# Two-level Strassen product with LoRA: M6 ahead of M7, T2 of the last four batches found early, U3 summed in SBUF

## The chip, the cores and the metric

One core of a Trainium2 chip runs the whole kernel. The metric is device time in microseconds (us), median of several runs.

## The reference, cut to what matters

```
# x (8, 512, 2048) f32; L0: A, B (8 adapters, rank 16); L1: W (2048, 2048), lora_A, lora_B (16 adapters, rank 16)
h = x + (x @ B0[i0].T) @ A0[i0].T          # per batch b: i0 = itok_B_3_7[b]
y = h + h @ W + (h @ A1[i1]) @ B1[i1]      # per batch b: i1 = itok_B_0_15[b]
```

The kernel computes y as x (I + W) plus low-rank terms, in f32 accuracy by splitting each operand in a high and a low part (w_hi, w_lo, b_hi, b_lo) with three matmuls for each product.

## The kernel before, in words

The product x (I + W) is found by the Winograd form of Strassen's method, with seven block products in place of eight. Batches are paired, so that the two batches of a pair stand side by side as the block matrix X11, X12, X21, X22 (half of the inner dimension, batch).

**First part (`one_level`), batches 0 to 3.** Two pairs p = 0, 1, each with products P1, P2, P6, P7, P4, P3, P5, each of 8 units. Unit n runs 24 matmuls (30 in P1, P2, P7, P4 of p = 0, which also find low-rank terms). All engines go through the same loop over n in their own queues. For unit n + 1 ScalarE casts the weight tile to `w_hi` (line 768) once TensorE has left unit n - 1, then VectorE finds `w_lo` (line 926); TensorE needs `w_lo` at the end of unit n. In the same way x is split (lines 779, 939). VectorE also adds the products up (line 987 and others) and forms sums of weights for the second part (`job_sum`, lines 1084 to 1094). SyncE issues loads in a written order: `load_raw` and `load_weights` for weights, `load_x` for x (X12 of pair 1 in P7 of pair 0). The four x tiles `x_raw[X11..X22]` each hold 8 chunks of 128x512.

**Second part (`two_level`), batches 4 to 7.** The four batches are multiplied by a two-level scheme: seven outer products in the order M1, M2, M7, M6, M4, M3, M5, each of seven inner products Q1 to Q7 in 14 units. Each outer product has an x block of four quarters `xq0` to `xq3` (1 MB each). For M7 the quarters are T3 = X12 - X22, for M6 T2 = T3 - X11, for M4 T2 + X21, for M5 T2 + X22. They are found by `first_diff` (line 2155), two adds or subtractions of 128x1024 for a quarter, from `xq` and a tile `tmp`; both are loaded by SyncE (`load_x`, line 1921, and `load_tmp`, line 1961). Three quarters are summed in the last units of the outer product ahead, the last one (quarter index 1) in unit 0. So that M6 can read T3 and M4 and M5 can read T2, GpSimd stores them to HBM (`store_t`, line 1856: `t3_kept`, three quarters, `t2_kept`, four).

Outer results: M1 begins U in `uq`, M2 is added in `stage` and stored. M7 is copied from PSUM by ScalarE into `stage` (line 2030, ten copies), the rest of its quarters added by VectorE (line 2214), and stored to two places of y (lines 1821, 1822). M6 is taken into `uq` (line 2211), and U2 is then added to the same two places of y by accumulating DMAs (`store_u2`, line 1834, 16 of 512 KB). M4 and M5 go the same way from `stage` (line 1825).

Weights come by `load_w` (line 1940), 1 MB for each inner product, two tiles in turn.

The order that the change touches is set by these lines:

```
M1, M2, M7, M6, M4, M3, M5 = range(7)
def x_kept(mo, i):   return i == 3 and mo in (M6, M4, M5)
def x_worked(mo, i): return mo in (M7, M6, M4, M5)
def by_act(q, begins): return begins and product(q)[0] in (M1, M7, M4, M5)
```

Of the kernel before, what the change touches and what calls it, by code (L numbers as in the profile page):

```python
# [43 lines left out]
M1, M2, M7, M6, M4, M3, M5 = range(7)  # L44
# [46 lines left out]
def one_level(nc, ctx, own, shared, xT, A0n, B0, W, A1, B1, yT):  # L91
# [176 lines left out]
    w_sum, w_ops, lrw, g_kept = shared.w_sum, shared.w_ops, shared.lrw, shared.g_kept  # L268
# [63 lines left out]
    job_summed = sem("job_summed")  # L332
    presum_done = sem("presum_done")
# [126 lines left out]
    def gpsimd(pool, early):  # L460
# [81 lines left out]
        for n in range(LAST + 1):  # L542
# [35 lines left out]
            if n in j_load_at:  # L578
                load_j(j_load_at[n])
            early(n)  # L580

    def sync(sp, early):
        def load_x(p, i, j):
            if p and i == X21:
                sp.wait_ge(w_ready, unit(0, P5, 4 + j) + 1)
                sp.wait_ge(f_stored[j], 16 * 4)
            elif p:
                user = {X11: P5, X12: P7, X22: P3}[i]
# [67 lines left out]

        def load_weights(n):
# [49 lines left out]
        for n in range(-1, LAST + 1):  # L707
# [188 lines left out]
    def vector(dve, early):  # L896
# [48 lines left out]
        def t3(p, j):  # L945
            dve.wait_ge(x_loaded[X12][j], 16 * (p + 1))
# [130 lines left out]

        def job_sum(o, k, e):
# [19 lines left out]
        for n in range(-1, LAST + 1):  # L1098
# [206 lines left out]
    part.g_stored = g_stored  # L1305
    part.u2_stored, part.u3_stored, part.stage_stored, part.stage_plan = u2_stored, u3_stored, stage_stored, stage_plan
# [6 lines left out]
def two_level(nc, ctx, own, shared, first, xT, B0, W, A1, yT):  # L1313
# [93 lines left out]
    def by_act(q, begins):  # L1407
        return begins and product(q)[0] in (M1, M7, M4, M5)
# [70 lines left out]
    for e, (mo, i, j) in enumerate(tmp_plan):  # L1479
        when = max(when, tmp_when[e - TMPS] if e >= TMPS else when, (unit(M6, 3) if mo in (M4, M5) else 0, 0))  # L1480
# [47 lines left out]
    j_split_at = {unit(M7, 12): 0, unit(M6, 1): 1, unit(M3, 11): 2, unit(M5, 0): 3}  # L1528
# [18 lines left out]
    t3_kept, t2_kept = (nc.dram_tensor(name, (4, P, 2, 2, N), F32).ap() for name in ("t3_kept", "t2_kept"))  # L1547
# [38 lines left out]
    x_stored = [sem(f"x_stored{i}") for i in range(4)]  # L1586
# [121 lines left out]
    def added_before(q, t, count, c, begins):  # L1708
# [5 lines left out]
        base = {M2: M1, M6: M1, M3: M6}.get(mo)  # L1714
# [48 lines left out]
    def gpsimd(pool):  # L1763
# [48 lines left out]
        def store_stage(mo, c, h):  # L1812
# [10 lines left out]
            else:  # L1823
                pool.wait_ge(u_stored[c], 16 * 4)
# [3 lines left out]
        def store_u2(c, h):  # L1828

            m = 4 * (c // 2) + 2 * h + 8  # L1830
            pool.wait_ge(*quarter_done(M6, c, 2 * h + 1))
            pool.wait_ge(stage_stored[GROUP[M7][c]][h], 16 * stage_stores(M7, c, h))
            for pair in (1, 0):
                pool.dma_start(y_at(batch(pair, c % 2), m), uq[:, c, 2 * h:2 * h + 2, :], accum_op=ALU.add
                               ).then_inc(u_stored[c], 16)
# [38 lines left out]
        def rest():  # L1874
            for n in range(LAST + 2):
# [4 lines left out]
                store_sums(early_sums(n))  # L1880
# [10 lines left out]
                store_sums(late_sums(n))  # L1891
# [5 lines left out]
                for i in range(len(lr_plan)):  # L1897
                    if n == (lr_split_of[i - 2] + 1 if i > 1 else unit(M7, 4 + 2 * i)):
# [4 lines left out]
    def sync(sp):  # L1903
        def load_x(mo, i):
# [12 lines left out]
            if mo == M6:  # L1917
                sp.wait_ge(x_stored[i], 16 * t_stores(M7, i))
                src = t3_kept[c]
# [22 lines left out]
        def load_tmp(e):  # L1942
# [33 lines left out]
        def rest():  # L1976
# [18 lines left out]
            for c in range(4):  # L1995
                sp.wait_ge(u_stored[c], 16 * 6)
# [130 lines left out]
    def vector(dve):  # L2127
# [17 lines left out]
        def first_diff(mo, i):  # L2145

            for j in range(2):
                if x_kept(mo, i):
                    dve.wait_ge(*x_split_done(product_at(mo - 1, Q3)))
                    if mo == M4:  # L2150
                        dve.wait_ge(x_stored[i], 16 * t_stores(M6, i))
                else:
# [3 lines left out]
                                         ALU.subtract if mo in (M7, M6) else ALU.add)  # L2156
            last.then_inc(x_summed, 1)

        def x_diff(kind, mo):
# [8 lines left out]
            if mo in (M7, M6) and kind != "t1":  # L2168
                dve.wait_ge(x_stored[dst], 16 * t_stores(mo, dst))
# [22 lines left out]
        def evict(q, t, count, c, begins):  # L2192
# [248 lines left out]
def lora_residual_program(nc, xT, ids0, ids1, A0n, B0, W, A1, B1, yT):  # L2441
# [4 lines left out]
    with ExitStack() as ctx:  # L2446
# [13 lines left out]

        shared.eye = sb("eye", [P, P])
# [85 lines left out]
```

## Time and profile before

| | |
|---|---|
| median of 3 runs | 1356.53 us (1356.39 to 1359.65) |
| the profiled execution | 1358.25 us |
| its span | 1356.3 us |
| TensorE busy | 1303.0 us (96%) |
| VectorE, ScalarE, GpSimd busy | 947.6, 459.1, 175.9 us |
| DMA | 321.57 MB, 237 GB/s over the span |

The span runs from the first to the last instruction. Engines in the rows: PE is TensorE, PEld its weight loads, DVE VectorE, ACT ScalarE, POOL GpSimd, SP SyncE. PEclk is the share of TensorE's full clock that was granted. "idle before" is how long an engine stood still ahead of an instruction, and what released it.

### The profile page before, as it was taken

To read this page: it belongs to the slowest core of one execution; us is meant where nothing else is said; L and a number is where in the kernel's file an instruction comes from. 1 tells how busy PE (TensorE), PEld (TensorE's weight loads), DVE (VectorE), ACT (ScalarE), POOL (GpSimd) and SP (SyncE) were. 2 spreads that over 40 slices of the span, in tenths; PEclk is the share of its full clock that TensorE was granted. 3 is DMA by queue.
4 is the path that set the end of the run, shared out by engine and by line. 5 is a ranking of instruction groups with operands and counts; after the bars stand their busy time and mean duration, and the time that the engine had idled before them with its cause. 6 is when DMAs were issued, how large, how long until landed. Compare 5 with 4: busy or idle time off the path is not lost.

```text
span 1356.3 us, 15438 instructions
## 1 busy us (share of the span) xinstructions
PE 1303.0 (96%) x5684; PEld 1070.4 (79%) x5684; DVE 947.6 (70%) x1025; ACT 459.1 (34%) x536; POOL 175.9 (13%) x304
## 2 busy tenths in 40 slices
PE   5999999998999999999999999999999889999996
PEld 4878888887878788878887888888888668888785
DVE  4454764455686876776578767886798767778995
ACT  2331232222332422232232443334444335443451
POOL 4100100011023110001202000011112200110022
PEclk8999999998999999999999999999999989999998
DMA  8873854368998965556978473598899997877377
GB/s 308 282 263 128 282 182 133 106 205 274 324 366 290 329 216 210 184 181 215 303 247 307 133 259 125 191 356 273 307 358 300 281 258 199 237 165 230 102 210 163
DMA packets 87823, 321.57 MB, mean 237 GB/s; under 512 B 15796, under 2 KB 15796, under 8 KB 80452
## 3 DMA queue, kind: packets, MB, share of 16 engines
q1 hardware_dynamic: 59188, 237.00, 51.1%
q0 software_dynamic: 28560, 83.58, 22.1%
q8 instruction: 46, 0.75, 0.2%
q14 instruction: 29, 0.24, 0.1%
HBM read 207.19 MB, written 114.36 MB: 237 GB/s over the span
## 4 chain that ended last, share of the span: by engine, by line
PE 68%; DVE 12%; DMA 12%; issue 3%; ACT 2%; SPq 1%; POOL 0%; DVEq 0%; POOLq 0%; ACTq 0%
PE ps L1266 31%; PE ps L2423 29%; PE ps L1239 2%; DMA w_sum<-w_raw 2%; PE ps L2379 2%; DMA wq<-w_ops 2%; DMA w_raw<-in_W 2%; DMA xq<-in_xT 2%; PE ps L1197 1%; ACT w_hi L768 1%; DMA x_raw<-in_W 1%; DVE w_lo L926 1%; DVE xq L2170 1%; DVE w_lo L2183 1%; DVE x_raw L912 1%
## 5 line engine op out<-in xcount | busy, mean ns | idle before, releaser
L1266 PE MATMUL ps<-b_hi,w_hi 128*128 128x512 f32 x896 | 351.8, 393 | 17.0 <-DVE w_lo L926 15.3
L1266 PE MATMUL ps<-b_lo,w_hi 128*128 128x512 f32 x896 | 350.4, 391 | 0.0
L1266 PE MATMUL ps<-b_hi,w_lo 128*128 128x512 f32 x896 | 350.0, 391 | 0.0
L2423 PE MATMUL ps<-b_hi,w_hi 128*128 128x512 f32 x784 | 308.6, 394 | 15.4 <-DVE w_lo L2183 12.7
L2423 PE MATMUL ps<-b_lo,w_hi 128*128 128x512 f32 x784 | 307.3, 392 | 0.0
L2423 PE MATMUL ps<-b_hi,w_lo 128*128 128x512 f32 x784 | 307.0, 392 | 0.0
L1266 PEld LDWEIGHTS ps<-b_hi,w_hi 128*128 128x128 f32 x896 | 169.4, 189 | 55.5 <-DVE w_lo L926 17.9
L1266 PEld LDWEIGHTS ps<-b_hi,w_lo 128*128 128x128 f32 x896 | 169.3, 189 | 35.6
L1266 PEld LDWEIGHTS ps<-b_lo,w_hi 128*128 128x128 f32 x896 | 169.3, 189 | 35.1
L2423 PEld LDWEIGHTS ps<-b_hi,w_hi 128*128 128x128 f32 x784 | 148.4, 189 | 50.0 <-DVE w_lo L2183 14.8
L2423 PEld LDWEIGHTS ps<-b_hi,w_lo 128*128 128x128 f32 x784 | 148.5, 189 | 31.3
L2423 PEld LDWEIGHTS ps<-b_lo,w_hi 128*128 128x128 f32 x784 | 148.6, 190 | 30.7
L2012 ACT CAST w_hi<-wq 128x1024 fp32r<-128x1024 f32 x98 | 103.2, 1053 | 188.7 <-PE ps L2423 165.2
L2183 DVE TENSOR_TENSOR w_lo<-wq,w_hi 128x1024 fp32r<-128x1024 f32 x98 | 119.5, 1220 | 57.5 <-ACT w_hi L2012 56.9
L926 DVE TENSOR_TENSOR w_lo<-w_raw,w_hi 128x1024 fp32r<-128x1024 f32 x48 | 58.7, 1224 | 101.5 <-ACT w_hi L768 101.3
L768 ACT CAST w_hi<-w_raw 128x1024 fp32r<-128x1024 f32 x48 | 50.6, 1054 | 218.9 <-PE ps L1239 112.9
L2189 DVE TENSOR_TENSOR b_lo<-xq,b_hi 128x1024 fp32r<-128x1024 f32 x98 | 119.5, 1219 | 5.8 <-ACT b_hi L2020 5.3
L2020 ACT CAST b_hi<-xq 128x1024 fp32r<-128x1024 f32 x98 | 102.9, 1050 | 43.5 <-DVE xq L2170 18.3
L768 ACT CAST w_hi<-x_raw 128x1024 fp32r<-128x1024 f32 x31 | 32.7, 1053 | 134.6 <-PE ps L1266 79.8
L926 DVE TENSOR_TENSOR w_lo<-x_raw,w_hi 128x1024 fp32r<-128x1024 f32 x31 | 38.0, 1224 | 52.3 <-ACT w_hi L768 52.3
L939 DVE TENSOR_TENSOR b_lo<-x_raw,b_hi 128x1024 fp32r<-128x1024 f32 x56 | 68.2, 1217 | 0.0
L2170 DVE TENSOR_TENSOR xq<-xq 128x2048 f32<-128x2048 f32 x28 | 63.9, 2282 | 0.0
(174 smaller groups left out, 1268.2 us busy)
## 6 DMA issues: line engine op xcount, KB each, us to landing
w_raw<-in_W SPq DMA_DIRECT2D x63, 512.0 KB, 6.7
wq<-w_ops SPq DMA_DIRECT2D x28, 1024.0 KB, 6.1
xq<-in_xT SPq DMA_DIRECT2D x44, 512.0 KB, 6.7
out_y<-stage POOLq DMA_DIRECT2D x40, 512.0 KB, 8.8
x_raw<-in_xT SPq DMA_DIRECT2D x32, 512.0 KB, 7.3
w_raw<-w_sum SPq DMA_DIRECT2D x25, 512.0 KB, 6.1
wq<-w_sum SPq DMA_DIRECT2D x12, 1024.0 KB, 8.7
out_y<-uq POOLq DMA_DIRECT2D x24, 512.0 KB, 14.1
```

What stands on the lines that cost most here:

```text
L768: act.copy(w_hi[n % 2][:, :, :], w_tile(n)[:, :, :]).then_inc(w_hi_done, 1)
L926: dve.tensor_tensor(w_lo[n % 2][:, :, :], w_tile(n)[:, :, :], w_hi[n % 2][:, :, :].bitcast(F32), ALU.subtract).then_inc(w_ready, 1)
L939: dve.tensor_tensor(b_lo[:, 2 * j:2 * j + 2, :], x_raw[i][:, 2 * j:2 * j + 2, :], b_hi[:, 2 * j:2 * j + 2, :].bitcast(F32), ALU.subtract). ...
L1239: last = pe.matmul(p_ps[:, :], a0[:, 2 * j + c, :], w[n % 2][:, c, :], start=(j == 0 and c == 0 and k == 0), stop=(j == 3 and c == 1 and k ...
L1266: last = pe.matmul(bank[:, :], w[n % 2][:, c, t * P:(t + 1) * P], x[:, 2 * j + c, :], start=(j == 0 and c == 0 and w is w_hi and x is b_hi ...
L2012: act.copy(w_hi[:, h, :, :], w_half(q, h)).then_inc(w_hi_done, 1)
L2020: act.copy(b_hi[:, 2 * (q % 2) + j, :, :], xq[x_use(q)[0]][:, j, :, :]).then_inc(x_hi_done, 1)
L2170: dve.tensor_tensor(xq[dst][:, :, :, :], xq[a][:, :, :, :], xq[b][:, :, :, :], ALU.subtract).then_inc(x_summed, 1)
L2183: dve.tensor_tensor(w_lo[:, h, :, :], w_half(q, h), w_hi[:, h, :, :].bitcast(F32), ALU.subtract).then_inc(w_ready, 1)
L2189: dve.tensor_tensor(b_lo[:, slot, :, :], xq[x_use(q)[0]][:, j, :, :], b_hi[:, slot, :, :].bitcast(F32), ALU.subtract).then_inc(x_ready, 1)
L2379: last = pe.matmul(lr_ps, cols, x[:, 2 * (q % 2) + c // 2, c % 2, :], start=(begins and c == 0 and x is b_hi), stop=(ends and c == 3 and x ...
L2423: last = pe.matmul(out, w[:, h, c, col:col + P], b[x], start=(po in (Q1, Q2, Q5, Q3) and c == 0 and i == 0), stop=(c == 3 and i == 2), ski ...
```

## The change

The diff does these things:

- The outer order is M1, M2, M6, M7, M4, M3, M5.
- T2 = X12 - X22 - X11 of batches 4 to 7 is found in the first part, in eight pieces of 128x1024 (`late_t2`), five in X12's tile during P7 of pair 0 (after units 25, 27, 28, 30 and 31) and three in X21's tile in P4 and P3 of pair 1 (after units 90, 93 and 96). A piece has three loads of 512 KB by SyncE, two subtractions by VectorE at the end of its loop body, and one store to `t2_kept` by GpSimd.
- Pair 1's X12 is loaded in P4 of pair 0, not in P7.
- M6 loads its four quarters from `t2_kept` as they are. M7 loads three quarters and keeps the fourth (T2 + X11). M4 now loads all four. `t3_kept`, `store_t` and its seven stores are gone.
- M7's ten beginning copies on ScalarE become VectorE adds of `uq`: `stage` = U2 + M7 = U3, stored twice as before. `store_u2` and its 16 accumulating DMAs are gone.

```diff
-M1, M2, M7, M6, M4, M3, M5 = range(7)
+M1, M2, M6, M7, M4, M3, M5 = range(7)
...
+    LATE_T2 = [(X12, unit(0, P7, 1)), (X12, unit(0, P7, 3)), (X12, unit(0, P7, 4)), (X12, unit(0, P7, 6)),
+               (X12, unit(0, P7, 7)), (X21, unit(1, P4, 2)), (X21, unit(1, P4, 5)), (X21, unit(1, P3, 0))]
...
+        def store_late_t2(s):
+            i, _ = LATE_T2[s]
+            pool.wait_ge(late_t2_summed, 2 * s + 2)
+            pool.dma_start(t2_kept[s // 2, :, s % 2, :, :], x_raw[i][:, 2 * (s % 2):2 * (s % 2) + 2, :]
+                           ).then_inc(late_t2_stored[s % 2], 16)
...
+            elif k == 0:
+                sp.wait_ge(late_t2_stored[j], 16 * (s // 2))
+            else:
+                sp.wait_ge(late_t2_summed, 2 * (s - 1) + k)
+            half, pair = ((0, 1), (1, 1), (0, 0))[k]
+            src = xT[4 + 2 * pair + s // 2 % 2, 2 * half + s // 4, :, s % 2, :, :]
+            sp.dma_start(x_raw[i][:, 2 * j:2 * j + 2, :], src).then_inc(x_loaded[i][j], 16)
...
-                if o == P7 and 2 <= u < 6:
-                    load_x(p + 1, X12, u - 2)
+                if (o, u) in ((P4, 1), (P4, 2), (P4, 3), (P4, 4)):
+                    load_x(p + 1, X12, (2, 0, 3, 1)[u - 1])
...
+        def late_t2(s):
...
+                    dve.wait_ge(x_loaded[i][j], came + 16 * late_t2_uses(i, j, s))
...
+                dve.tensor_tensor(tiles[0], tiles[0], tiles[k], ALU.subtract).then_inc(late_t2_summed, 1)
...
-        return i == 3 and mo in (M6, M4, M5)
+        return i == 3 and mo in (M7, M5)
...
-        return mo in (M7, M6, M4, M5)
+        return mo in (M7, M4, M5)
...
-        return begins and product(q)[0] in (M1, M7, M4, M5)
+        return begins and product(q)[0] in (M1, M4, M5)
...
-        base = {M2: M1, M6: M1, M3: M6}.get(mo)
+        base = {M2: M1, M6: M1, M7: M6, M3: M6}.get(mo)
...
-                        if qmo == M6:
-                            store_u2(c, t // 2)
...
-                src = t3_kept[c]
+                for j in range(2):
+                    sp.wait_ge(first.late_t2_stored[j], 16 * (first.LATE_T2S // 2))
+                src = t2_kept[c]
```

How the rows of the queues move, at three places. First VectorE's queue from the last unit of P7 into P4 of pair 0 (`u` is the tile that sums products up, `q` a low-rank sum). Before:

```order
L926 TENSOR_TENSOR w_lo<-w_raw,w_hi 128x1024
L939 TENSOR_TENSOR b_lo<-x_raw,b_hi 128x1024
L1004 TENSOR_TENSOR a_lo<-lr_raw,a_hi 128x256
L987 TENSOR_TENSOR u<-ps,u 128x512 x4
L1062 TENSOR_TENSOR q<-ps,q 128x512
L921 TENSOR_TENSOR w_raw<-w_raw,eye 128x128 x2
L926 TENSOR_TENSOR w_lo<-w_raw,w_hi 128x1024
```

Now:

```order
L974 TENSOR_TENSOR w_lo<-w_raw,w_hi 128x1024
L987 TENSOR_TENSOR b_lo<-x_raw,b_hi 128x1024
L1052 TENSOR_TENSOR a_lo<-lr_raw,a_hi 128x256
L1035 TENSOR_TENSOR u<-ps,u 128x512 x3
L1136 TENSOR_TENSOR x_raw<-x_raw 128x1024 x2
L1035 TENSOR_TENSOR u<-ps,u 128x512
L1110 TENSOR_TENSOR q<-ps,q 128x512
L969 TENSOR_TENSOR w_raw<-w_raw,eye 128x128 x2
L974 TENSOR_TENSOR w_lo<-w_raw,w_hi 128x1024
```

The two subtractions of piece 4 stand ahead of a partial sum, the low-rank sum and the weights' split for unit 33.

Second, SyncE's queue through P7 of pair 0. Before:

```order
L625 DMA w_raw<-w_sum 128x1024 x5
L591 DMA x_raw<-in_xT 128x1024
L625 DMA w_raw<-w_sum 128x1024
L591 DMA x_raw<-in_xT 128x1024
L625 DMA w_raw<-in_W 128x1024
```

Now:

```order
L653 DMA w_raw<-w_sum 128x1024 x3
L699 DMA x_raw<-in_xT 128x1024 x3
L653 DMA w_raw<-w_sum 128x1024 x2
L699 DMA x_raw<-in_xT 128x1024 x3
L653 DMA w_raw<-w_sum 128x1024
L653 DMA w_raw<-in_W 128x1024
L699 DMA x_raw<-in_xT 128x1024 x3
L653 DMA w_raw<-in_W 128x1024
L699 DMA x_raw<-in_xT 128x1024 x3
```

Each single x load gave way to three, with waits on the piece ahead, between the weight loads.

Third, GpSimd's queue in the second part, from the end of M7 into M6 before:

```order
L1821 DMA out_y<-stage 128x1024
L1822 DMA out_y<-stage 128x1024
L1856 DMA t_kept<-xq 128x2048
L1821 DMA out_y<-stage 128x1024
L1822 DMA out_y<-stage 128x1024
L1834 DMA out_y<-uq 128x1024 x2
L1789 DMA lr_raw_q<-lrw 128x1x512
```

and from M6 into M7 now:

```order
L1868 DMA j_raw_q<-g_kept 16x4x16 x4
L1898 DMA out_y<-fix 128x1024 x2
L1847 DMA lr_raw_q<-lrw 128x1x512
L1898 DMA out_y<-fix 128x1024 x2
L1879 DMA out_y<-stage 128x1024
L1880 DMA out_y<-stage 128x1024
```

The stores of `xq` and `uq` are gone. The two stores of each `stage` pair now come in the block just ahead of M4.

## Rows read from the trace of the kernel before

**Rows 1.** The page: engine totals, and TensorE's busy tenths in 40 equal slices.
```profile
PE 1303.0 (96%) x5684; PEld 1070.4 (79%) x5684; DVE 947.6 (70%) x1025; ACT 459.1 (34%) x536; POOL 175.9 (13%) x304
...
PE   5999999998999999999999999999999889999996
```

**Rows 2.** Busy time by stretch: length, each engine's us (instructions), PEclk, DMA share, GB/s.
```profile
182.00:242.00 60.00, 60.00 (x266) 49.68 (x265) 30.77 (x39) 15.34 (x20) 1.12 (x2) 1.00 0.38 124
604.00:660.00 56.00, 54.85 (x242) 45.40 (x243) 35.92 (x39) 14.83 (x17) 10.35 (x20) 1.00 0.75 246
905.00:990.00 85.00, 84.51 (x373) 69.63 (x373) 64.76 (x63) 35.79 (x42) 12.01 (x22) 1.00 0.82 296
990.00:1060.00 70.00, 69.29 (x305) 56.80 (x304) 64.24 (x62) 32.10 (x39) 16.59 (x24) 1.00 0.98 312
1060.00:1080.00 20.00, 19.11 (x85) 15.49 (x83) 14.85 (x17) 5.06 (x5) 6.11 (x7) 1.00 1.05 285
1080.00:1100.00 20.00, 14.36 (x51) 11.58 (x52) 13.71 (x12) 7.38 (x8) 0.72 (x1) 0.74 1.05 284
1100.00:1120.00 20.00, 16.26 (x60) 12.88 (x59) 10.13 (x9) 5.74 (x6) 1.73 (x2) 0.83 0.89 244
1120.00:1140.00 20.00, 20.00 (x90) 16.55 (x89) 14.33 (x16) 11.13 (x15) 0.71 (x1) 1.00 0.60 182
```

**Rows 3.** Waits from 1068 to 1125 us: who waited for what, total, times, longest.
```profile
PE ps L2423 <- DVE w_lo L2183: 10.3, 2, 6.5
ACT w_hi L2012 <- DMA wq<-w_ops: 10.2, 1, 10.2
ACT b_hi L2020 <- DVE xq L2155: 9.8, 1, 9.8
DVE xq L2155 <- DMA xq<-in_xT: 5.9, 1, 5.9
```

**Rows 4.** The chain that ended last, within 1065 to 1095 us: start, length, what.
```profile
1061.72 20.35 DMA xq<-in_xT
...
1085.61 21.71 DMA wq<-w_ops
```

**Rows 5.** DMA issues from 1060 to 1110 us: how many, KB each, median us to landing.
```profile
out_y<-uq POOLq DMA_DIRECT2D x7, 512.0 KB, 28.8
tmp<-t_kept SPq DMA_DIRECT2D x4, 512.0 KB, 19.9
```

**Rows 6.** DMA issues from 900 to 985 us, and all that they moved.
```profile
DMA packets 5880, 25.17 MB, mean 296 GB/s; under 512 B 1027, under 2 KB 1027, under 8 KB 4595
...
out_y<-stage POOLq DMA_DIRECT2D x14, 512.0 KB, 9.7
tmp<-in_xT SPq DMA_DIRECT2D x8, 512.0 KB, 7.4
```

**Rows 7.** Groups by line and shape, whole span: total us, mean ns, idle before.
```profile
L2155 DVE TENSOR_TENSOR xq<-xq,tmp 128x1024 f32<-128x1024 f32 x32 | 37.6, 1217 | 5.9 <-DMA xq<-in_xT 5.9
...
L2214 DVE TENSOR_TENSOR stage<-ps,uq 128x1024 f32<-128x1024 f32 x6 | 7.3, 1220 | 5.0 <-PE ps L2423 5.0
```

**Rows 8.** VectorE's timeline, P7 into P4 of pair 0: start, us, line, instruction, idle before.
```profile
238.62 1.23 DVE L926 TENSOR_TENSOR w_lo<-w_raw,w_hi 128x1024 fp32r<-128x1024 f32 x1 [3.70 <-ACT w_hi L768]
...
246.59 1.22 DVE L926 TENSOR_TENSOR w_lo<-w_raw,w_hi 128x1024 fp32r<-128x1024 f32 x1 [1.17 <-ACT w_hi L768]
...
252.22 1.23 DVE L926 TENSOR_TENSOR w_lo<-w_raw,w_hi 128x1024 fp32r<-128x1024 f32 x1 [2.73 <-ACT w_hi L768]
```

**Rows 9.** VectorE's timeline in P4 and P3 of pair 1: the splits of units 94 and 95, then a low-rank sum.
```profile
629.28 1.22 DVE L926 TENSOR_TENSOR w_lo<-x_raw,w_hi 128x1024 fp32r<-128x1024 f32 x1 [2.90 <-ACT w_hi L768]
...
635.48 1.23 DVE L926 TENSOR_TENSOR w_lo<-w_raw,w_hi 128x1024 fp32r<-128x1024 f32 x1 [1.17 <-ACT w_hi L768]
...
662.15 1.22 DVE L1033 TENSOR_TENSOR lr_raw<-lr_raw,stage_all 128x1024 f32<-128x1024 f32 x1
```

**Rows 10.** GpSimd's timeline there: the loads that this low-rank sum waits for.
```profile
649.36 1.94 POOL L498 DMA_DIRECT2D stage_all<-lrw  x4
```

More of the change, by code:

```diff
@@ L124, in keep_unit, with late_t2_uses @@
         return unit(0, P5 if use >= UNITS else P3, use % UNITS)
+    LATE_T2 = [(X12, unit(0, P7, 1)), (X12, unit(0, P7, 3)), (X12, unit(0, P7, 4)), (X12, unit(0, P7, 6)),
+               (X12, unit(0, P7, 7)), (X21, unit(1, P4, 2)), (X21, unit(1, P4, 5)), (X21, unit(1, P3, 0))]
+    late_t2_at = {n: s for s, (_, n) in enumerate(LATE_T2)}
+    late_t2_loads = {(s, k): (s % 2, 2, 3)[k] for s in range(len(LATE_T2)) for k in range(3)}
+    def late_t2_uses(i, j, s):
+        return sum(LATE_T2[t][0] == i and slot == j for (t, _), slot in late_t2_loads.items() if t <= s)
     raw_of, raw_plan = {}, []
@@ L332, in one_level @@
     job_summed = sem("job_summed")
+    late_t2_summed = sem("late_t2_summed")
+    late_t2_stored = [sem(f"late_t2_stored{j}") for j in range(2)]
     presum_done = sem("presum_done")
@@ L586, in load_x @@
                 sp.wait_ge(f_stored[j], 16 * 4)
+            elif p and i == X12:
+                if j < 2:
+                    sp.wait_ge(late_t2_stored[j], 16 * sum(k == X12 for k, _ in LATE_T2[j::2]))
+                else:
+                    sp.wait_ge(late_t2_summed, 2 * sum(k == X12 for k, _ in LATE_T2) - 3 + j)
             elif p:
-                user = {X11: P5, X12: P7, X22: P3}[i]
+                user = {X11: P5, X22: P3}[i]
                 sp.wait_ge(x_ready, 4 * ((p - 1) * PRODUCTS + user) + j + 1)
@@ L743, in sync @@
                     load_second(m)
+            for s, (i, done) in enumerate(LATE_T2):
+                if n == (LATE_T2[s - 1][1] + 1 if s and LATE_T2[s - 1][0] == i else done - 1):
+                    for k in range(3):
+                        load_late_t2(s, k)
             if n + 3 in place_of:
@@ L1076, in fix @@
                               ).then_inc(fix_done, 1)
+        def late_t2(s):
+            i, _ = LATE_T2[s]
+            came = 16 * {X12: 1, X21: 2 + 4}[i]
+            tiles = [x_raw[i][:, 2 * j:2 * j + 2, :] for j in (s % 2, 2, 3)]
+            for k in (1, 2):
+                for t in ((0, 1), (2,))[k - 1]:
+                    j = late_t2_loads[s, t]
+                    dve.wait_ge(x_loaded[i][j], came + 16 * late_t2_uses(i, j, s))
+                if k == 2:
+                    dve.wait_ge(late_t2_summed, 2 * s + 1)
+                dve.tensor_tensor(tiles[0], tiles[0], tiles[k], ALU.subtract).then_inc(late_t2_summed, 1)
         def job_sum(o, k, e):
@@ L1183, in vector @@
                 job_sum(*use)
+            if n in late_t2_at:
+                late_t2(late_t2_at[n])
             early(n)
@@ L1479, in two_level @@
     for e, (mo, i, j) in enumerate(tmp_plan):
-        when = max(when, tmp_when[e - TMPS] if e >= TMPS else when, (unit(M6, 3) if mo in (M4, M5) else 0, 0))
+        when = max(when, tmp_when[e - TMPS] if e >= TMPS else when, (0, 0))
         tmp_issue.setdefault(when, []).append(e)
@@ L1546, in two_level @@
     w_ops, w_sum, lrw, g_kept = shared.w_ops, shared.w_sum, shared.lrw, shared.g_kept
-    t3_kept, t2_kept = (nc.dram_tensor(name, (4, P, 2, 2, N), F32).ap() for name in ("t3_kept", "t2_kept"))
+    t2_kept = shared.t2_kept
     eye, ids, j_hi, j_lo = shared.eye, shared.ids, shared.j_hi, shared.j_lo
@@ L1823, in store_stage @@
             else:
-                pool.wait_ge(u_stored[c], 16 * 4)
+                pool.wait_ge(stage_stored[GROUP[M7][c]][h], 16 * stage_stores(M7, c, h))
                 pool.dma_start(y_at(other if mo == M5 else one_pair, m + 8), tiles, accum_op=ALU.add
                                ).then_inc(stored, 16)
[L1828 to L1835, printed above, removed]
         def store_fin(c, h):
@@ L2155, in first_diff @@
                 last = dve.tensor_tensor(xq[i][:, j, :, :], xq[i][:, j, :, :], tmp_tile((mo, i, j))[:, :, :],
-                                         ALU.subtract if mo in (M7, M6) else ALU.add)
+                                         ALU.subtract if mo == M7 and not x_kept(mo, i) else ALU.add)
             last.then_inc(x_summed, 1)
@@ L2202, in evict @@
             target = stage[:, GROUP[mo][c]] if mo in GROUP else uq[:, c]
-            if begins and mo == M2:
+            if begins and mo in (M2, M7):
                 for pair in stage_free(mo, c, t // 2):
```

52 lines of the change are left out of this document (21 added, 31 removed).

## The prediction, made before the changed kernel ran

> **What bounds the kernel now.** I read the page first [rows 1]: TensorE is busy for 1303.0 of 1356.3 us, so its idle time is what can be won, and its slices show where: two neighbouring slices of 40 (each 34 us), the 32nd and 33rd, stand at 8, in the second part. The table by stretch [rows 2] gives the size. An undisturbed stretch of 20 us holds 90 matmuls (1120 to 1140), so one costs 20 / 90 = 0.222 us. From 1060 to 1120 us there are 85, 51 and 60, which is 270 - 196 = 74 too few, and 74 x 0.222 = 16.4 us lost. The granted clock there is 0.74 and 0.83 of full, a mixture of the levels 2.4 and 1.2 GHz. The DMA engines are full: share 1.05, 1.05, 0.89.
>
> The waits of that stretch [rows 3] name the causes. TensorE waited 10.3 us, in two waits, for `w_lo` from VectorE. Behind the first wait VectorE stood 5.9 us for a quarter of M4's x, and behind the second ScalarE stood 10.2 us for a weight tile. The chain of work [rows 4] shows the same two transfers: 20.35 us for x and 21.71 us for the weights. The issues [rows 5] show who filled the engines: the accumulating stores of U2 (`out_y<-uq`) took 28.8 us to land, and `tmp` 19.9. One product earlier, from 900 to 985 us, the same kind of `tmp` load landed in 7.4 us and plain stores of `stage` in 9.7 [rows 6]. So the stall at the start of M4 is transfers that land 12 us too late, in a queue that M6 filled.
>
> **What the second part gains.** Of M6 and M7 together the change removes 16 accumulating stores (8.4 MB), seven stores of `xq` (7.3 MB) and eight `tmp` loads (4.2 MB), and adds two loads of 0.5 MB. What stands just ahead of M4 is now M7. Counting a 128x1024 tile as 0.524 MB, M7 issues 16 stores of `stage` (8.4 MB), eight loads of M4's x (4.2), eight of `tmp` (4.2), seven weight tiles (7.3) and about 1.5 MB of low-rank rows: 25.6 MB. This is the load that the old M7 had: 25.17 MB from 900 to 985 us [rows 6], with the engines at 0.82 and TensorE busy for 84.51 of 85 us from 905 to 990 [rows 2]. I take that row as the price: nearly all of the 16.4 us comes back and about 0.5 us stays. Bounds: all of it and the waits of M7 and M6 too, (85 - 84.51) + (70 - 69.29) = 1.2 us more, is -17.6; half of it, if M7's 16 stores still crowd the entry of M4, is -8.2.
>
> VectorE does not gain in the second part. It drops M6's eight subtractions (8 x 1.217 = 9.7 us) and takes the ten beginnings of M7 from ScalarE, six of 128x1024 at 1.220 us and four of half the size, about 10 us [rows 7]. In the new M6 and M7 it carries what it carried in the old M6: 64.24 of 70 us, where TensorE still ran for 69.29 [rows 2]. So I cost this move at nothing. Its cover is 5.8 us in 70; if that went, each us of VectorE's lateness would be one of TensorE's.
>
> The first of my two looks at a rule: after the two waits the clock in rows 2 is below full, and the second, 10.3 - 6.5 = 3.8 us of waiting [rows 3], cost 30 missing matmuls, 6.7 us, in its stretch [rows 2]. The Trainium skill says the same (TensorE: Matmul & The Clock Gate, HAM oscillation): a TensorE that stood waiting for a DMA resumes at the low clock, so that a wait costs more than its length. By the wait alone the gain would be 10.3 us, by the matmul count it is 16.4; the count decides. It speaks against the change in the first part, where a new wait would be charged in the same way.
>
> **What the first part pays.** Eight pieces bring 24 loads (12.6 MB), 8 stores (4.2 MB) and 16 subtractions, 16 x 1.22 = 19.5 us of VectorE. They lie beside TensorE as long as VectorE still finds each `w_lo` in time.
>
> P7 of pair 0, 182 to 242 us: VectorE is busy for 30.77 of 60 us, the DMA engines at 0.38 with 124 GB/s [rows 2], 7.4 MB. Five pieces add 10.5 MB, the moved X12 loads take 2.1 away: 15.8 MB in 60 us is 264 GB/s, under the 296 at which `tmp` landed in 7.4 us. The tight place is piece 4. Its second and third loads wait for piece 3, whose two subtractions (2.4 us) fill the idle time that begins 3.70 us before 238.62, behind 0.5 us of diagonal adds: they end near 236.9. Piece 4's own come after the split at 238.62, a split of x, a small one and three partial sums, near 243.1 us. With a landing of 7.4 us the data is there at 244.3 and they end at 246.7. From 243.1 to the split of unit 33 at 246.59 there were 3.5 us, 0.6 of them idle, so that split now begins at 249.6 and ends at 250.8. TensorE needs it when unit 32 ends: the split at 252.22 waited for that end with a cast of 1.05 us between, so it was at 251.1 [rows 8]. That leaves 0.3 us to spare. I take 0.5 us for the risk; from 0 to 3 (2.0 us late if they land in 9.7 us as the stores did, plus the clock).
>
> P4 and P3 of pair 1, 604 to 660 us: 13.8 MB in 56 us, 6.3 MB come on top, 358 GB/s; at 246 GB/s the share was 0.75, so this is a full queue for a while. VectorE has 56 - 35.9 = 20 us free for 7.3 us. After piece 6 the split of unit 95 comes 2.4 us later than 635.48, at 637.9; TensorE ends unit 94 about 639.0 (two units of 5.44 us after 628.1, when the cast ahead of 629.28 began), so 0.1 us is lost [rows 9]. VectorE then hands the last partial sum on 2.4 us later, the low-rank loads that were issued from 649.36 to 651.3 us [rows 10] start 2.4 us later, and share the queue. They are used at 662.15 with no wait before it [rows 9]. With 7.4 us they land at 661.1, with 9.7 at 663.4. I take 1.0 us for the three pieces; from 0 to 4.
>
> **The queues.** SyncE waits for VectorE's piece s - 1 ahead of the loads of piece s; behind it stand the weight loads, which run four units ahead in pair 0 and about three in pair 1, 15 us or more against 7.4 us of landing: nothing. GpSimd waits for the pieces ahead of partial stores, whose `stage` tiles are needed many units later: nothing, except as counted in pair 1. M7's `stage` tiles have all of M6 between them and their stores of M2. ScalarE only loses work. Pair 1's X12 comes in P4, still 20 units ahead of its use.
>
> **Sum.** -16.4 + 0.5 (entry of M4) + 0.5 + 0.1 + 0.9 (first part) = -14.4 us. The profiled execution took 1358.25 us, so the same kind of execution would take 1343.9. That execution lies 1.7 us above the median of the runs, 1356.53, and against this the forecast is **1342.1 us**. A measurement of this kernel can tell about 0.3%, 4.1 us, from no change.
>
> **Rivals.**
> 1. *The entry of M4 keeps half of its stall* (chance 0.12). M7's 16 stores are now next to M4, and four of them come in its last two units, with the last x quarter that M4 waits for. For it: the 16 loads for M4 fall in the same units. Against it: rows 2 and 6, the same load without a stall. -8.2 + 2 = -6.2: 1350.3 us.
> 2. *Slower: T2's loads hold up VectorE* (0.05). VectorE works in order, so a subtraction that waits for its load holds the weights' split behind it. Pieces 2 and 4 have their loads issued only one unit ahead. If these landed in 19.9 us [rows 5] in place of 7.4, each would cost TensorE about 12 us, and piece 3 and 7 some: 2 x 12 + 3 for the clock - 16.4 + 0.5 = +11: 1367.6 us. It decides from a landing of some 15 us on (2 x 8 us past the margins). Against it is the 0.38 of rows 2 in P7. Of the transfers in rows 5 those of SyncE were slow while GpSimd's filled the engines. The Trainium skill states why (DMA: Bandwidth & Descriptors, Issuing engines are not separate DMA queues): the DMAs of all issuers run on the same 16 engines and interleave. By that rule T2's 16.8 MB slow whatever shares their time; by the rows there is room in P7 and little in pair 1, where my 1.0 us is its price.
> 3. *It does not do what it says* (0.03): the x quarter for M4 can be asked for only when the old one has been split, two to three units ahead, and might be late whatever M6 stored. Then little changes: -1 + 1.5, 1357 us. Against it: landings of 7.4 us against 20.35.
>
> **Chances.** Forecast 0.80, its own range 1338.9 (the bound -17.6) to 1348 (first part at its upper bounds); rivals 0.12, 0.05, 0.03. The range of 8 in 10 reaches into rival 1: 1338 to 1350. Faster by over 0.3% (below 1352.5): 0.80 + 0.12 = 0.92. Within 0.3%: 0.03. Slower: 0.05.
>
> **What would show it.** Right: TensorE with 88 or more matmuls in each 20 us around the entry of M4, clock 1.00; no row `out_y<-uq` of accumulating stores with 28.8 us; DMA share below 1 in M6 and M7; `xq` and `wq` loads near M4 landing in 6 to 10 us; new VectorE rows `x_raw<-x_raw` x16 at 1.22 us with under 5 us of idle in front; TensorE waiting under 2 us in pair 0's P7 and P4 and under 3 in pair 1's P4 and P3. Wrong: a wait of TensorE over 3 us at the entry of M4 (rival 1), or VectorE rows of `late_t2` idle for a DMA, with TensorE behind (rival 2).

## The result: about half of the forecast gain, and where the rest went

The changed kernel takes 1349.84 us (median of 7 runs, 1347.17 to 1350.99) against 1356.53 us (7 runs). The ratio is 0.9938, with a 95% interval of 0.9927 to 0.995: 0.6% faster. That is 6.7 us by the two medians and 8.4 us by the ratio, of 14.4 us forecast. The forecast was 1342.1 us, the range 1338 to 1350. The profiled execution took 1349.26 us, its span 1347.6 us; it is compared with the profile before, span 1356.3 us.

The page of the changed kernel, engine totals and TensorE's busy tenths, answers to [rows 1]:

```profile
PE 1299.9 (96%) x5684; PEld 1067.8 (79%) x5684; DVE 965.6 (72%) x1043; ACT 451.6 (34%) x526; POOL 162.5 (12%) x289
...
PE   5999999998999999999899999999999999999996
```

The two 8s of the 32nd and 33rd slice are gone. A new 8 stands in the 20th slice, from 640 to 674 us. The table by stretch, with the columns of [rows 2], gives both their size:

```profile
660.00:680.00 20.00, 15.26 (x55) 12.02 (x54) 8.35 (x9) 3.52 (x4) 4.71 (x10) 0.83 0.95 326
1060.00:1080.00 20.00, 20.00 (x90) 16.57 (x89) 17.16 (x22) 6.12 (x6) 3.16 (x6) 1.00 1.02 406
1080.00:1100.00 20.00, 20.00 (x90) 16.57 (x89) 18.43 (x15) 10.01 (x11) 1.75 (x3) 1.00 0.85 316
1100.00:1120.00 20.00, 20.00 (x89) 16.54 (x89) 14.27 (x14) 9.37 (x11) 2.48 (x3) 1.00 0.71 168
```

At the entry of M4 TensorE now runs 90, 90 and 89 matmuls where it ran 85, 51 and 60, at full clock. The first matmul of the second part started at 741.7 us before and starts at 749.7 now: the first part lost 8.0 us. The last matmul of the kernel started at 1344.6 us before and starts at 1335.9 now, so the second part gained 8.7 + 8.0 = 16.7 us; 8.7 us is also the difference of the spans (1356.3 - 1347.6). Of the 8.0 us, 7.3 lie in the first line above: 55 matmuls where before there were 88, 33 x 0.222 us.

The DMA issues of the changed kernel from 1060 to 1110 us, beside [rows 5]:

```profile
DMA packets 3871, 15.51 MB, mean 310 GB/s; under 512 B 608, under 2 KB 608, under 8 KB 3352
...
out_y<-stage POOLq DMA_DIRECT2D x10, 512.0 KB, 6.7
tmp<-t_kept SPq DMA_DIRECT2D x6, 512.0 KB, 6.8
```

The plain stores land in 6.7 us where the accumulating ones took 28.8, and `tmp` in 6.8 where it took 19.9. The engines' share is still 1.02 from 1060 to 1080 us, but at 406 GB/s and not 285: a share of 1 is two different loads.

The new stall is in pair 1 of the first part. Its waits (changed kernel, 630 to 676 us: who waited for what, total, times, longest):

```profile
PE ps L1280 <- DVE val L1103: 4.7, 1, 4.7
...
POOL stage_all L513 <- DMA out_y<-stage_all: 4.6, 1, 4.6
DVE lr_raw L1081 <- DMA stage_all<-lrw: 4.6, 1, 4.6
```

And the chain of work there (start, length, what):

```profile
644.76 0.70 DVE stage_all L1026
645.45 0.28 issue
645.74 0.54 POOL out_y L541
646.28 0.06 issue
646.34 9.28 DMA out_y<-stage_all
...
656.13 1.44 POOL stage_all L513 x3
657.57 9.64 DMA stage_all<-lrw
667.21 0.03 issue
```

Read from the bottom: TensorE waits for a low-rank value, this for the low-rank rows `lrw`, loaded into the tile `stage_all`; GpSimd may load them only when what stood in that tile has been stored. Before, the four stores of that tile landed in 4.5 us (median), so that the loads of [rows 10] followed at 649.36 with no wait. GpSimd's timeline of the kernel before has the first of them at:

```profile
643.42 1.14 POOL L526 DMA_DIRECT2D out_y<-stage_all  x2 [18.00 <-DVE stage_all L978]
```

Now it is issued at 645.74, 2.3 us later, and the stores land in 9.3 us.

Who filled the queue? SyncE's timeline of the changed kernel (start, us, issue):

```profile
629.92 6.80 SPq L699 DMA_DIRECT2D x_raw<-in_xT  x3
636.83 0.37 SPq L725 DMA_DIRECT2D w_raw<-w_sum  x1
637.24 0.43 SPq L730 DMA_DIRECT2D w_ops<-w_raw  x1
637.71 0.50 SPq L730 DMA_DIRECT2D w_ops<-x_raw  x1
638.32 1.11 SPq L725 DMA_DIRECT2D w_more<-w_sum  x1
```

and the same issues in the kernel before:

```profile
626.45 0.46 SPq L681 DMA_DIRECT2D w_raw<-w_sum  x1
632.80 0.32 SPq L686 DMA_DIRECT2D w_ops<-w_raw  x1
633.94 0.32 SPq L686 DMA_DIRECT2D w_ops<-x_raw  x1
634.69 0.32 SPq L681 DMA_DIRECT2D w_more<-w_sum  x1
```

The three loads of piece 7 took SyncE 6.80 us, since the second and third wait for the subtractions of piece 6, which VectorE ends at 636.4 us:

```profile
633.81 2.55 DVE L1136 TENSOR_TENSOR x_raw<-x_raw 128x1024 f32<-128x1024 f32 x2
```

A weight load (issued at 626.45 before) and the stores of weight sums (from 632.80 before) stood behind them, and came in one bunch from 636.8 us. The Trainium skill says where such a wait is served (DMA: Bandwidth & Descriptors, Anatomy of one DMA — SWDGE (gpsimd) path): on the issuing sequencer, ahead of the dispatch, and not in the DMA engines. That section follows GpSimd's DMAs; the rows above show the same for SyncE, whose next issue came at 636.83 us, after the 6.80 us.

### The profile page after: what moved, and what is told of

It is laid out like the page before. It is cut to its first block, busy times and chain, and to the rows that moved or that the text cites. A ratio compares the mean times of both kernels' runs of the same rounds, so it can differ in the third digit from the quotient of the medians.

```text
span 1347.6 us, 15432 instructions
## 1 busy us (share of the span) xinstructions
PE 1299.9 (96%) x5684; PEld 1067.8 (79%) x5684; DVE 965.6 (72%) x1043; ACT 451.6 (34%) x526; POOL 162.5 (12%) x289
## 4 chain that ended last, share of the span: by engine, by line
PE 68%; DVE 14%; DMA 11%; issue 3%; ACT 2%; SPq 1%; POOL 0%; DVEq 0%; ACTq 0%; POOLq 0%
PE ps L2450 33%; PE ps L1328 28%; DMA w_sum<-w_raw 3%; PE ps L1301 2%; PE ps L2406 2%; DMA w_raw<-in_W 2%; DMA stage_all<-lrw 2%; ACT w_hi L816 1%; DVE w_lo L974 1%; DMA x_raw<-in_W 1%; DMA out_y<-stage_all 1%; DVE xq L2197 1%; PE ps L1259 1%; DVE b_lo L2216 1%; DVE w_lo L2210 1%
```

## The experiments

Each kernel was timed together with the kernel before, on one chip; the chip was not the same in all series. What a variant of the changed kernel gives back is counted below from its median to the changed kernel's, 1349.84 us, of another series. By the ratios to the kernel before the amounts are 1 to 3 us smaller, and a ratio is known to within 2 to 4 us, so the traces carry the argument about pair 1 and the times support it. Theory and rivals for the 8 us in pair 1: the pieces make VectorE hand over late (a start 2.4 us later); their bytes fill the DMA engines; their place in SyncE's queue holds other transfers up. For the 16.7 us in the second part: the bytes that are gone, or the accumulation.

### Smaller subtractions in pieces 6 and 7

```diff
-                dve.tensor_tensor(tiles[0], tiles[0], tiles[k], ALU.subtract).then_inc(late_t2_summed, 1)
+                few = slice(0, 16) if s >= 6 else slice(0, N)
+                dve.tensor_tensor(tiles[0][:, :, few], tiles[0][:, :, few], tiles[k][:, :, few], ALU.subtract
+                                  ).then_inc(late_t2_summed, 1)
```

> The subtractions of pieces 6 and 7 work on 16 of 512 columns (their T2 is left incomplete), loads and stores stay whole. Theory V: VectorE hands the last partial sum of P4 on 2.4 us late, and the late low-rank loads follow from that; then the wait of 4.9 us before the low-rank matmul at 667 us falls to about 0.2, and the time by 8 us, to some 1342. Rival D: the transfers of the pieces fill the DMA engines, and the chain is late with or without VectorE; then the wait stays at 3 us or more and the time at 1347 to 1350.

Measured: 1343.9 us (1340.11 to 1344.27), ratio 0.9907 (0.9889 to 0.9925). 5.9 us come back (4.2 by the ratios). Relative to VectorE's work the store of `stage_all` is issued nearly as early as in the kernel before (14.4 and 14.1 us in the table at the end of this section), yet it lands in 9.1 us, about as slowly as in the changed kernel, and GpSimd waits for it:

```profile
650.99 1.94 POOL L513 DMA_DIRECT2D stage_all<-lrw  x4 [3.62 <-DMA out_y<-stage_all]
```

### Smaller loads in pieces 6 and 7

```diff
-            sp.dma_start(x_raw[i][:, 2 * j:2 * j + 2, :], src).then_inc(x_loaded[i][j], 16)
+            few = slice(0, 64) if s >= 6 else slice(0, N)
+            sp.dma_start(x_raw[i][:, 2 * j:2 * j + 2, few], src[:, :, few]).then_inc(x_loaded[i][j], 16)
```

> The six loads of pieces 6 and 7 bring 64 of 512 columns (their T2 is left incomplete), subtractions and stores stay whole. Rival D: the stage store lands in 5 us or less instead of 9.3, the low-rank loads in about 7, the wait is under 1 us and the time near 1342. Theory V: the low-rank loads start 2.4 us late all the same, the wait stays at 2 to 3 us (plus the clock if it is long enough), time 1345 to 1348.

Measured: 1344.79 us (1343.47 to 1347.93), ratio 0.9919 (0.9897 to 0.994). Here 5.1 us come back (2.6 by the ratios), and here too the landing stays, at 9.0 us, though 2.8 MB of loads are gone. TensorE waits 2.6 us, as Theory V said, but neither theory had a slow landing in both kernels: it is made neither by VectorE's lateness alone nor by the bytes of the pieces' loads alone.

### Pieces 6 and 7 moved later

```diff
-                (X12, unit(0, P7, 7)), (X21, unit(1, P4, 2)), (X21, unit(1, P4, 5)), (X21, unit(1, P3, 0))]
+                (X12, unit(0, P7, 7)), (X21, unit(1, P4, 2)), (X21, unit(1, P3, 4)), (X21, unit(1, P5, 1))]
...
+            if mo == M1 and i >= 2:
+                for j in range(2):
+                    sp.wait_ge(first.late_t2_stored[j], 16 * (first.LATE_T2S // 2))
```

> Nothing is left out: pieces 6 and 7 move from after units 93 and 96 to after units 100 and 105, behind the low-rank loads. Both theories: the wait at 667 us is 0.2 to 1 us as in the kernel before, the 8 us of the first part come back, 1341 to 1343 us. If the loss has another cause in pair 1 (the jobs' sums, the weights), the wait moves to another place and the time stays at 1347 or more.

Measured: 1341.82 us (1340.34 to 1344.89), ratio 0.9893 (0.9875 to 0.9912). 8.0 us come back (6.1 by the ratios), with no work left out. `stage_all` lands in 4.3 us, GpSimd issues the loads with no wait, and 660 to 680 us holds its 88 matmuls:

```profile
650.71 1.94 POOL L513 DMA_DIRECT2D stage_all<-lrw  x4
```

### Plain stores of U2 in the kernel before

```diff
-                pool.dma_start(y_at(batch(pair, c % 2), m), uq[:, c, 2 * h:2 * h + 2, :], accum_op=ALU.add
+                pool.dma_start(y_at(batch(pair, c % 2), m), uq[:, c, 2 * h:2 * h + 2, :]
```

> The kernel before, with the 16 stores of U2 as plain stores, not accumulating ones (y is then short of M7's share). Theory R: the stall at M4's entry comes from the accumulation, which keeps the engines busy for more than its bytes; then these stores land in 6 to 10 us rather than 17 to 29, TensorE's waits there (10.3 us) fall under 2 and the time to about 1342. Rival B: it is the number of bytes; then half or more of the stall stays, 1349 to 1356.

Measured: 1341.58 us (1339.32 to 1342.62), ratio 0.9888 (0.9867 to 0.9908): 14.5 us come back with the old order, every store and every `tmp` load still there. Its stretches:

```profile
1060.00:1080.00 20.00, 19.43 (x86) 15.79 (x85) 18.60 (x20) 7.32 (x8) 3.17 (x6) 1.00 1.03 391
1080.00:1100.00 20.00, 20.00 (x90) 16.56 (x89) 17.52 (x16) 8.69 (x10) 2.47 (x3) 1.00 0.91 282
```

And its DMA issues from 1020 to 1110 us:

```profile
DMA packets 7287, 28.14 MB, mean 313 GB/s; under 512 B 1457, under 2 KB 1457, under 8 KB 6259
...
out_y<-uq POOLq DMA_DIRECT2D x12, 512.0 KB, 12.4
...
tmp<-t_kept SPq DMA_DIRECT2D x6, 512.0 KB, 9.6
```

The kernel before, the same view:

```profile
DMA packets 6825, 26.02 MB, mean 289 GB/s; under 512 B 1378, under 2 KB 1378, under 8 KB 5929
...
out_y<-uq POOLq DMA_DIRECT2D x14, 512.0 KB, 23.4
...
tmp<-t_kept SPq DMA_DIRECT2D x6, 512.0 KB, 16.8
```

With plain stores more bytes pass in the same 90 us, and each lands in little more than half the time.

### Small stores of T3 and T2 in the kernel before

```diff
-            pool.dma_start((t2_kept if mo == M6 else t3_kept)[X_QUARTER[i]], xq[i][:, :, :, :]
+            pool.dma_start((t2_kept if mo == M6 else t3_kept)[X_QUARTER[i]][:, :, :, 0:64], xq[i][:, :, :, 0:64]
...
-                src = t3_kept[c]
...
-                src = t2_kept[c, :, j, :, :]
+                src = xT[batch(0, c % 2), c // 2, :, j, :, :]
```

> The kernel before, with the seven stores of T3 and T2 cut to 64 of 512 columns; M6, M4 and M5 read x from its first place in the same sizes (their blocks are then not T2), so 7.3 MB of stores are out of M7 and M6, and U2 still accumulates. If accumulation alone makes the stall (the plain stores of U2 took all 16.4 us away), most of it stays: TensorE waits 6 us or more at M4's entry and the time is 1348 to 1356. If every MB counts alike, these 7.3 MB are worth about as much as U2's 8.4 and the time is near 1342.

Measured: 1357.76 us (10 runs, 1355.85 to 1361.37), ratio 1.0005 (0.9992 to 1.0018). Nothing: the stall stands where it stood.

```profile
1080.00:1100.00 20.00, 14.28 (x55) 11.33 (x54) 12.29 (x11) 7.37 (x8) 2.21 (x3) 0.83 1.05 285
```

### Small accumulating stores of U2 in the kernel before

```diff
-                pool.dma_start(y_at(batch(pair, c % 2), m), uq[:, c, 2 * h:2 * h + 2, :], accum_op=ALU.add
-                               ).then_inc(u_stored[c], 16)
+                pool.dma_start(y_at(batch(pair, c % 2), m)[:, :, 0:64], uq[:, c, 2 * h:2 * h + 2, 0:64],
+                               accum_op=ALU.add).then_inc(u_stored[c], 16)
```

> The kernel before, with the 16 accumulating stores of U2 cut to 64 of 512 columns (y is then short of U2). Both theories: the stall at M4's entry is gone, 1341 to 1343 us. If it gives the same time as the plain stores of U2 did (1341.6), the 8.4 MB themselves cost nothing there and only the accumulation did.

Measured: 1344.12 us (1341.64 to 1345.93), ratio 0.9897 (0.9874 to 0.9921). An eighth of the bytes, still accumulating, gives what all the bytes give when stored plainly; the two intervals overlap. In both, TensorE waits 0.6 us at the entry of M4 in place of 10.3. So the 8.4 MB alone cost nothing that shows, and accumulating an eighth of them cost little or nothing; the times cannot tell, at 2.5 us between the medians. The price was that of accumulating all 8.4 MB.

### Pieces later, and pair 1's X22 later

This takes the kernel with pieces 6 and 7 moved, and looks at the wait of some 4 us near 320 us, which stands in all kernels.

```diff
-                if o == P3 and 2 <= u < 6:
-                    load_x(p + 1, X22, u - 2)
+                if o == P3 and 4 <= u < 8:
+                    load_x(p + 1, X22, u - 4)
```

> The version with pieces 6 and 7 moved, and pair 1's X22 loaded from units P3 4 to 7 of pair 0, not 2 to 5: 1 MB less beside the low-rank loads that TensorE waits for at 320 us (4.3 us and a stretch at the low clock, in the kernel before too). If that wait is of the same kind as the one that the change brought to pair 1, the loads land in 7 to 8 us rather than 10, the wait falls to 1 to 2 us, and the time to 1337 to 1340. If they wait for something else, 1341.8 stays.

Measured: 1343.84 us (1339.46 to 1347.27), ratio 0.9894 (0.9872 to 0.9915): no different from 1341.82 without the edit. TensorE's wait is 3.5 us in place of 4.1. The rows came in 9.0 us in place of 9.3, in stretches of 35 us with 8.15 and 8.90 MB, so the two x loads that were moved away were not what made them slow. What does stays open.

```profile
PE ps L1280 <- DVE val L1103: 3.5, 1, 3.5
```

### SyncE held in the kernel before, nothing else

The first three experiments left one suspect, SyncE's queue. This kernel adds one wait to the kernel before, and neither a byte nor a subtraction.

```diff
+            if n == unit(1, P4, 6):
+                sp.wait_ge(w_ready, n + 2)
             if n + 3 in place_of:
                 load_weights(n + 3)
```

> The kernel before with one wait more: ahead of the weight loads of unit 94's loop body SyncE waits until VectorE has split unit 95's weights, at about 636.7 us. No byte and no subtraction is added. In the changed kernel SyncE stood from 629.9 to 636.8 us in the three loads of piece 7 (they wait for the subtractions of piece 6), where before it issued at 632.8 us. Theory A, the hold counts: the stores of weight sums and loads that stood behind come in one bunch from 636.7 us, the DMA engines are idle just before and full until 656 us, the stores of stage_all land in 7 us or more in place of 4.5, GpSimd waits for them, and up to 1 us of wait appears near 667 us: 1357 to 1359 us. Theory B, the delay is made of the pieces' bytes and VectorE's time alone: landing 4.5 us, no wait of GpSimd, 1356.5 us as before. By either the time moves little, since VectorE's stores are not late here; the landing tells.

Measured: 1363.77 us (1363.23 to 1364.63), ratio 1.0051 (1.0034 to 1.0068): 7 us slower. I had expected the landing, but not that it would reach TensorE. SyncE's timeline:

```profile
638.30 0.32 SPq L681 DMA_DIRECT2D w_raw<-w_sum  x1
638.67 0.43 SPq L686 DMA_DIRECT2D w_ops<-w_raw  x1
```

The DMA engines from 634 to 656 us (busy tenths in 40 slices, what they moved, a store's landing):

```profile
DMA  0000000003798899999999999899999999999999
...
DMA packets 1629, 5.85 MB, mean 266 GB/s; under 512 B 204, under 2 KB 204, under 8 KB 1627
...
out_y<-stage_all POOLq DMA_DIRECT2D x4, 256.0 KB, 9.8
```

GpSimd, TensorE's wait and its stretch:

```profile
655.89 1.93 POOL L498 DMA_DIRECT2D stage_all<-lrw  x4 [4.95 <-DMA out_y<-stage_all]
```

```profile
PE ps L1220 <- DVE val L1057: 4.0, 1, 4.0
```

```profile
660.00:680.00 20.00, 16.05 (x64) 12.79 (x63) 8.74 (x10) 4.14 (x5) 4.72 (x10) 0.91 0.87 285
```

The engines stand idle for the first nine slices (5 us) and are full for the rest; the kernel before moved 6.31 MB there against 5.85 now, and its store landed in 4.5 us. The stall of the changed kernel is here in all its parts, a little smaller (64 matmuls in its stretch and not 55), with none of its work.

### Piece 7's loads behind SyncE's other issues

The other way round: the changed kernel with all bytes and all subtractions, and the three loads at the end of the loop body.

```diff
             for s, (i, done) in enumerate(LATE_T2):
-                if n == (LATE_T2[s - 1][1] + 1 if s and LATE_T2[s - 1][0] == i else done - 1):
+                if s < 7 and n == (LATE_T2[s - 1][1] + 1 if s and LATE_T2[s - 1][0] == i else done - 1):
...
             for use in job_sums.get(n - 1, []):
                 store_job(*use)
+            if n == LATE_T2[6][1] + 1:
+                for k in range(3):
+                    load_late_t2(7, k)
```

> The changed kernel with the three loads of piece 7 issued at the end of unit 94's loop body in place of ahead of its weight load and stores of weight sums. The same bytes, the same VectorE work. Theory A, SyncE's hold makes the bunch: the stores of weight sums go out near 633 us, stage_all lands in about 5 to 7 us in place of 9.3, and half or more of the 4.9 us wait at 667 us goes: 1344 to 1347 us. Theory B, bytes and VectorE's time: the landing stays near 9 us, the wait stays, 1349.8 us.

Measured: 1342.77 us (5 runs, 1342.14 to 1351.94), ratio 0.9909 (0.9877 to 0.994). The median is 7.1 us below the changed kernel's, but one of the five runs took 1351.94 us, and the intervals of the two ratios overlap; the trace says it plainly. The stall is gone:

```profile
628.12 0.56 SPq L725 DMA_DIRECT2D w_raw<-w_sum  x1
634.49 0.32 SPq L730 DMA_DIRECT2D w_ops<-w_raw  x1
635.62 0.32 SPq L730 DMA_DIRECT2D w_ops<-x_raw  x1
635.99 2.43 SPq L699 DMA_DIRECT2D x_raw<-in_xT  x3
```

```profile
654.03 1.94 POOL L513 DMA_DIRECT2D stage_all<-lrw  x4 [0.82 <-DMA out_y<-stage_all]
```

```profile
660.00:680.00 20.00, 19.92 (x89) 16.14 (x88) 11.32 (x12) 4.70 (x5) 4.72 (x10) 1.00 1.00 361
```

89 matmuls at full clock, beside DMA engines that are full (1.00, 361 GB/s). Full engines by themselves were not the trouble. Even while the stores of `stage_all` are under way, 647.4 to 654.0 us, the engines stand at 1.03 with 357 GB/s, and the stores land in 6.2 us; in the kernel with SyncE held they stand at 1.03 with 370 GB/s, and the stores land in 9.8. The difference must lie in what was still queued when the stores came. No run here shows that queue.

### Both cuts at once, SyncE's queue as it is

The two small-size edits of the first two experiments together.

> The changed kernel with both cuts at once: pieces 6 and 7 load 64 of 512 columns and subtract 16 of 512; every wait and every issue is still there. Their T2 is wrong in the other columns. The first two runs gave back 5.9 us (subtractions) and 5.1 us (loads) of 8. If the two are two ways into one chain (a late start and a slow landing), both together give at most what moving the pieces gave: 1341.8 us, and the wait at 664 us is gone (under 0.5 us). If the queue's hold and issues themselves cost something, it stays above: 1343 to 1345 us.

Measured: 1343.29 us (1342.46 to 1344.83), ratio 0.99 (0.9883 to 0.9917). The time can't be told from that of the pieces moved later, but TensorE still waits 0.8 us, and `stage_all` still lands in 8.8 us. With an eighth of the loads' bytes and next to none of the subtractions' time, the hold is still seen in the landing; the store now starts early enough to absorb most of it.

### The series side by side

SyncE's issue of the load and the store behind piece 7, and the issue of the first store of `stage_all`, in us after the start of VectorE's split of unit 94; then what follows. Each is from one profile; the time is the median of the runs. "GpSimd waits" is its wait for the landing, "TensorE waits" the wait for the low-rank value.

| kernel | load | store | `stage_all` out | lands in | GpSimd waits | TensorE waits | us |
|---|---|---|---|---|---|---|---|
| before | -2.8 | 3.5 | 14.1 | 4.5 | 0 | 0 | 1356.5 |
| changed | 7.6 | 8.0 | 16.5 | 9.3 | 4.6 | 4.7 | 1349.8 |
| small subtractions | 5.7 | 6.1 | 14.4 | 9.1 | 3.6 | 1.2 | 1343.9 |
| small loads | 7.6 | 8.0 | 16.5 | 9.0 | 4.1 | 2.6 | 1344.8 |
| both small | 5.8 | 6.2 | 14.4 | 8.8 | 3.9 | 0.8 | 1343.3 |
| pieces moved later | -2.9 | 3.5 | 14.2 | 4.3 | 0 | 0 | 1341.8 |
| piece 7's loads behind | -2.9 | 3.5 | 16.5 | 6.2 | 0.8 | 0 | 1342.8 |
| before, SyncE held | 7.4 | 7.8 | 14.1 | 9.8 | 5.0 | 4.0 | 1363.8 |

The landings fall into two groups, and the load and store columns alone divide them: 4.3 to 6.2 us where SyncE issued in time, 8.8 to 9.8 where it was held. Within the groups other things count too: the 6.2 is that of the kernel with all the pieces' work still in pair 1. VectorE's lateness, the 2.4 us from 14.1 to 16.5, costs TensorE nothing by itself (piece 7's loads behind); the hold costs 7 us by itself (before, SyncE held). The small subtractions help since the subtractions are what the loads wait for, which ends the hold 1.9 us sooner, and since the store starts 2.1 us earlier. The small loads leave both as they were and still shorten TensorE's wait; there the loads of the low-rank rows landed in 7.9 us in place of the 9.6 of the chain above. That fewer bytes beside them are the reason is likely, but not shown.

Pieces 6 and 7 moved later, and piece 7's loads behind, both compute all of y, in 1341.8 and 1342.8 us; no measurement here tells them apart. The first is faster than both kernels beyond the intervals. The second is faster than the kernel before beyond its interval, and than the changed kernel by its median and in four of its five runs.

## Why the prediction was half right

The measured 1349.84 us lies inside the range of 1338 to 1350, but by luck. The forecast's own range ended at 1348; the rest was there for Rival 1, and what made the time was neither the forecast nor Rival 1 but a stall in pair 1, priced at 1.0 us.

**The entry of M4: right, by the price I named.** The terms -16.4 + 0.5 stand against 16.7 us measured in the whole second part, and TensorE waits for nothing from 1060 to 1130 us. The row of the old M7 [rows 6], taken as the price of the new one, held: stores of `stage` in 6.7 us (9.7 there), `tmp` in 6.8 (7.4 there). But I counted megabytes removed, and the runs say that most of what I counted was worthless: the stores of T3 and T2 gave nothing (1.0005) as long as U2 accumulated, while the accumulation alone gave 14.5 us. The sign of it stood in [rows 2]: a share of 1.05 moved 285 GB/s, and a share of 0.82 moved 296. I read the first as "full" and not as "slow for its bytes".

**VectorE in the second part: right.** M7's beginnings as adds cost nothing that a stretch shows; TensorE was busy for 84.55 us of the 85 from 905 us and for 69.30 of the 70 from 990 (84.51 and 69.29 before).

**P7 of pair 0: right on the mechanism, 0 in place of 0.5 us.** The three loads of each piece landed in 6.0 us, and VectorE waited for one once, 2.0 us, with TensorE unmoved. The 16 subtractions took 19.5 us in all, as counted:

```profile
L1136 DVE TENSOR_TENSOR x_raw<-x_raw 128x1024 f32<-128x1024 f32 x16 | 19.5, 1221 | 2.7 <-DMA x_raw<-in_xT 2.0
```

**P4 and P3 of pair 1: the step that failed.** The prediction said "With 7.4 us they land at 661.1, with 9.7 at 663.4. I take 1.0 us for the three pieces; from 0 to 4." The term measured 7.3 us in its own stretch (8.0 in the whole first part), outside its own bounds. VectorE's 2.4 us were right to the tenth (16.5 - 14.1). Two things were missing. The low-rank loads do not start when VectorE is done, but when the tile's store has landed, so that two landings stand in series and a slower queue counts twice: 9.3 + 9.6 us. The prediction had the loads start 2.4 us late, near 651.8 us; they started at 656.1. And the sentence on the queues, "behind it stand the weight loads, which run four units ahead in pair 0 and about three in pair 1, 15 us or more against 7.4 us of landing: nothing", asked only whether the held transfers come too late for their own use. They did not. They came all at once, ahead of the store on which GpSimd waited, and with the hold that store landed in 8.8 to 9.8 us. The hold itself was in reach: piece 7's second and third loads wait for piece 6's subtractions, which I had placed after the split of unit 94, and SyncE's queue shows the stores of weight sums behind them.

**The clock.** Of 7.3 us lost, 4.7 are the wait; the rest, 2.6 us, is lost in the same stretch, whose granted clock is 0.83. The prediction charged the old stall so and said that a new wait would be charged in the same way, but its bound of 4 us held no such term. The Trainium skill's rule (TensorE: Matmul & The Clock Gate, HAM oscillation), that a TensorE which waited for a DMA resumes at the low clock, agrees with both stalls: 0.83 here, and 0.74 and 0.83 at the entry of M4 before.

**The rivals.** Rival 1 gave nearly the measured time, 1350.3, but by a mechanism that did not come: M4 kept nothing of its stall. Rival 3, that little changes at the entry of M4, did not come either. Rival 2, T2's loads holding up VectorE, did not come; but it was next to the truth, since it was T2's loads that held a queue up, and the queue was SyncE's. The rule I cited there, that the DMAs of all issuers share 16 engines (the Trainium skill, DMA: Bandwidth & Descriptors, Issuing engines are not separate DMA queues), fits what the kernel with SyncE held shows: a wait in SyncE's queue slowed GpSimd's stores from 4.5 to 9.8 us. Of the signs listed, the one that failed is that TensorE would wait under 3 us in pair 1's P4 and P3; it waited 4.7.

## What to carry to other kernels

When a DMA with a wait is put in front of others in an issuing queue, ask what the held transfers will land on when they are let go, and not only whether they are late for their own use; put it behind the issues that could go now. A tile that is stored and then loaded again makes two landings in series, so when landings grow its slack must cover the growth of both. Where DMA engines are full at far fewer GB/s than elsewhere in the same kernel (here 285 against 406), look for accumulating transfers before counting bytes.

## What the runs showed of the hardware

- 16 accumulating stores of 512 KB took 14.5 us more of this kernel's time than plain ones in their place. The plain ones could not be told in time from accumulating ones of an eighth of the size. The landing was 23.4 us against 12.4 from 1020 to 1110 us. With accumulation in the queue the engines moved 284 GB/s at a share of 1.05; without it 391 at 1.03 and 406 at 1.02.
- One more wait in SyncE's queue left the DMA engines idle for 5 us and then full for 17, and GpSimd's 256 KB stores landed in 9.8 us in place of 4.5, though fewer bytes were moved in the 22 us (5.85 and 6.31 MB). The kernel took 7 us longer.
